# Variance products of two norms as four 64x64 tiles, with one logarithm and one exponential for both, and a new order of work

## The reference

```python
x1 = x + layernorm(attention(x)) * n1g + n1b
y  = x1 + layernorm(fc2(gelu(fc1(x1)))) * n2g + n2b
# layernorm(v) = (v - mean(v)) / sqrt(var(v) + 1e-5), over the 64 channels
```

## Time and profile before

| | |
|---|---|
| median of 3 runs | 8857.75 us (8851.5 to 8859.13) |
| profiled execution: time | 8850.95 us |
| profiled execution: span | 8849.2 us |
| mean granted TensorE clock | 0.967 |
| TensorE matmul busy | 8401.3 us, 95% |
| ScalarE busy | 6230.1 us, 70% |
| VectorE busy | 5742.6 us, 65% |
| GpSimd busy | 5155.6 us, 58% |

### The profile page before, as it was taken

How to read it: one execution, slowest core, us unless ns; L and a number is a source line. 1 busy time by engine, 2 the same in 40 slices (tenths; PEclk the granted TensorE clock), 3 DMA queues, 4 the chain that set the end, 5 groups by cost and what they waited for, 6 DMA issues and landing times.

```text
span 8849.2 us, 652880 instructions
## 1 busy us (share of the span) xinstructions
PE 8401.3 (95%) x291636; PEld 5471.0 (62%) x291636; DVE 5742.6 (65%) x8029; ACT 6230.1 (70%) x8530; POOL 5155.6 (58%) x5127
## 2 busy tenths in 40 slices
PE   8799999999999999999999999999999999878686
PEld 5556666666666666666666666666666666557565
DVE  1457777777777777777777777777777777222121
ACT  1468888888888888888888888888888888322121
POOL 0357777777777777777777777777777777100000
PEclk9789999999999999999999999999999999889888
DMA  3111111111111111111111111111111111699999
GB/s 99 39 32 38 37 38 38 38 38 37 38 38 38 38 38 37 38 37 35 36 38 37 38 38 38 38 37 38 38 38 38 37 37 36 202 324 319 337 317 332
DMA packets 1105192, 700.01 MB, mean 79 GB/s; under 512 B 616850, under 2 KB 1026834, under 8 KB 1100948
## 3 DMA queue, kind: packets, MB, share of 16 engines
q1 hardware_dynamic: 1100484, 564.33, 23.9%
q10 hardware_dynamic: 4608, 134.22, 3.5%
HBM read 412.97 MB, written 285.21 MB: 79 GB/s over the span
## 4 chain that ended last, share of the span: by engine, by line
PE 93%; DMA 4%; issue 1%; SPq 0%; POOL 0%; DVE 0%; ACTq 0%; ACT 0%; POOLq 0%; DVEq 0%
PE ps L475 15%; PE ps L453 13%; PE ps L511 12%; PE ps L523 11%; PE ps L436 10%; PE ps L551 10%; PE ps L501 6%; PE ps L487 5%; PE ps L495 5%; PE ps L424 3%; DMA out<-arena 3%; PE ps L398 1%; PE ps L389 1%; PE ps L390 1%; SPq L262 0%
## 5 line engine op out<-in xcount | busy, mean ns | idle before, releaser
L475 PEld LDWEIGHTS ps<-arena 32*32 32x32 f32 x131072 | 1290.9, 104 | 541.8 <-issue 508.4
L475 PE MATMUL ps<-arena 32*32 32x16 f32 x131072 | 1425.4, 186 | 17.9 <-issue 12.6
L664 ACT ACTIVATE arena<-ps,arena 128x1024 f32<-128x1024 f32 x1024 | 1140.4, 1114 | 357.8 <-PE ps L523 205.9
L775 DVE TENSOR_TENSOR arena<-ps,arena 128x768 f32<-128x768 f32 x1024 | 962.1, 940 | 539.3 <-PE ps L436 539.3
L913 POOL TENSOR_TENSOR arena<-arena 128x512 f32<-128x512 f32 x512 | 536.9, 1049 | 1282.9 <-DVE arena L846 1009.9
L453 PEld LDWEIGHTS ps<-arena 32*32 32x32 f32 x131072 | 1167.1, 105 | 152.6 <-issue 152.6
L453 PE MATMUL ps<-arena 32*32 32x16 f32 x131072 | 1218.9, 180 | 34.3 <-issue 34.3
L960 POOL TENSOR_TENSOR arena<-arena 128x512 f32<-128x512 f32 x512 | 629.5, 1230 | 1037.6 <-DVE arena L827 1037.6
L551 PE MATMUL ps<-xch,amat 128*128 128x256 f32 x4096 | 924.6, 388 | 288.0 <-ACT arena L688 214.3
L511 PE MATMUL ps<-arena 64*128 64x512 f32 x4096 | 1178.9, 652 | 8.6 <-ACT arena L664 4.5
L922 POOL TENSOR_TENSOR arena<-arena 128x512 f32<-128x512 f32 x1024 | 1044.0, 1041 | 10.5 <-PE ps L475 10.4
(11 more groups left out here) (89 smaller groups left out, 14021.8 us busy)
## 6 DMA issues: line engine op xcount, KB each, us to landing
arena<-in_x SPq DMA_DIRECT2D x4096, 32.0 KB
y<-ystripe SPq DMA_DIRECT2D x256, 512.0 KB, 5.3
amat<-mix SPq DMA_DIRECT2D x512, 256.0 KB, 3.4
xch<-y SPq DMA_DIRECT2D x512, 256.0 KB, 4.0
out<-arena ACTq DMA_DIRECT2D x32, 4096.0 KB, 27.1
mix<-amat SPq DMA_DIRECT2D x64, 256.0 KB, 2.0
wri<-in_w_real SPq DMA_DIRECT2D x64, 64.0 KB, 1.8
wri<-in_w_imag SPq DMA_DIRECT2D x64, 64.0 KB, 1.9
```

What stands on the lines that cost most here:

```text
L475: ins = mm(PV[32 * h:32 * h + 32, b, c0:c0 + N], vexp[r, sl, h, :, :], pT[r, sl, h // 2, h % 2, :], start=True, stop=True, tile_position=( ...
L664: f(hT[kk], M, ACT.Gelu, bias=b1[:, kk:kk + 1]).then_inc(done, 1)
L775: tt(qkv[ring(g, 4)][:, :, 4 * pp:4 * pp + 4, :].rearrange("p w s n -> p s w n"), M.rearrange("p a (s n) -> p (a s) n", s=2)[:, :, 0:3 * C ...
```

## The change

- Both variances come in one piece, `variances(i4, i6)`: four 64x64 products on the four quarters of the array. For the first norm the halves of `sq1` are swapped before, by two DMAs of 128 KB that SP issues (`swap_halves`, four groups behind the load), so that its products use the off-diagonal quarters; the second norm's use the diagonal ones. The results go to banks 0 and 1.
- One logarithm and one exponential over 1024 columns (`logs`, `roots`) replace two of 512 each.
- PSUM is laid out anew: `MA` in banks 0 and 1 (turned input, variances, first half of the first layer), `MB` in 2 and 3 (qkv products, second half), `PV` in the lower halves of 4 and 5 with the scores in their upper halves, `D1` in 6 and `H2` in 7.
- The orders of TensorE, ScalarE, VectorE and GpSimd change. The two parts of `scores` now stand in different steps, the two of `first_layer` side by side; softmax and weighted sum come one step earlier. Waits follow the new layout.

```diff
+SWAP = 4
-        sq1, l1, r1, dn1, x1T = (carve(512) for _ in range(5))
-        sq2, l2, r2, dn2, yg = (carve(512) for _ in range(5))
+        sq1, sq1x, dn1, x1T = (carve(512) for _ in range(4))
+        ls, rts = carve(1024), carve(1024)
+        r1, r2 = rts[:, 0:512], rts[:, 512:1024]
+        sq2, dn2, yg = (carve(512) for _ in range(3))
...
-        M = ps[:, 0:2, :]
-        S = ps[:, 2, :]
-        PV = ps[:, 3:5, 0:256]
-        PA = ps[:, 3, :]
-        D1, H2, TR = ps[:, 5, :], ps[:, 6, :], ps[:, 7, :]
-        XT, V1, V2 = D1, TR, PA
+        MA, MB = ps[:, 0:2, :], ps[:, 2:4, :]
+        PV = ps[:, 4:6, 0:256]
+        D1, H2 = ps[:, 6, :], ps[:, 7, :]
+        VV = MA
+        V1, V2 = VV[:, 0, :], VV[:, 1, :]
+        XT = MA[:, 0, :]
+        def S(sl):
+            return ps[:, 4 + sl // 4, 256:512]
...
+            def swap_halves(g):
+                if there(g):
+                    need(sp, sq1_sb, g)
+                    for a in range(2):
+                        sp.dma_start(sq1x[a * C:a * C + C, :], sq1[(1 - a) * C:(2 - a) * C, :]).then_inc(sq1x_in, 16)
...
                     load_x(d * 2 + k // GPS, k % GPS, Group(d * 8, k))
+                    swap_halves(Group(d * 8, k - SWAP))
                     if k % GPS == 0:
                         store_y(d * 2 + (k // GPS - 3), Group(d * 8, k - 12 + GPS - 1))
...
-                        after(pe, (dn1_sb, i5), (xT_sb, before(g)))
+                        after(pe, (gelu0, i6), (logs_sb, i5, i7), (xT_sb, before(g)))
...
-                            need(pe, biased, before(g))
+                            after(pe, (oT_sb, i3), (biased, before(g)))
...
-                            after(pe, (l2_sb, i7), (oT_sb, before(g)))
+                            after(pe, (biased, i2), (oT_sb, before(g)))
...
-                        after(pe, (xT_sb, i0), (dn1_sb, before(g)))
+                        need(pe, dn1_sb, before(g))
...
-                def variance1(g):
-                    if there(g):
-                        need(pe, sq1_sb, g)
-                        need(pe, l1_sb, before(g))
-                        mm(V1, ones, sq1, start=True, stop=True).then_inc(var1_ps, 1)
...
+                def variances(g, h):
+                    if there(g) or there(h):
+                        need(pe, sq1x_in, g, 32)
+                        need(pe, sq2_sb, h)
+                        after(pe, (xT_sb, i0), (gelu0, i6), (logs_sb, before(g), before(h)))
+                        settled(pe)
+                        if there(g):
+                            for a in range(2):
+                                b = 1 - a
+                                ins = mm(V1[b * C:b * C + C, :], ones[a * C:a * C + C, a * C:a * C + C],
+                                         sq1x[a * C:a * C + C, :], start=True, stop=True, tile_position=(a * C, b * C))
+                        if there(h):
+                            for a in range(2):
+                                ins = mm(V2[a * C:a * C + C, :], ones[a * C:a * C + C, a * C:a * C + C],
+                                         sq2[a * C:a * C + C, :], start=True, stop=True, tile_position=(a * C, a * C))
+                        ins.then_inc(var_ps, 1)
...
-                            after(pe, (gelu1, i6), (qkvB_sb, i1), (qkvA_sb, i1), (gelu0, before(g)))
+                            after(pe, (logs_sb, i4, i6), (xT_sb, i0), (gelu0, before(g)))
...
                 turn_x(i0)
-                weighted(i4, 0, pvA_ps)
-                first_layer(i5, 0, fc1a_ps)
-                weighted(i4, 1, pvB_ps)
+                scores(i2, 1)
                 second_layer(i6, 0, fc2a_ps)
                 second_layer(i6, 1, fc2b_ps)
-                project(i4)
-                project_qkv(i0, 0, qkvA_ps)
-                variance2(i6)
-                variance1(i4)
-                project_qkv(i0, 1, qkvB_ps)
-                scores(i2, 0)
-                scores(i2, 1)
-                first_layer(i5, 1, fc1b_ps)
+                project_qkv(i0, 0, MB, qkvA_ps)
+                weighted(i3, 0, pvA_ps)
+                variances(i4, i6)
+                project_qkv(i0, 1, MB, qkvB_ps)
+                weighted(i3, 1, pvB_ps)
+                first_layer(i5, 0, MA, fc1a_ps)
+                first_layer(i5, 1, MB, fc1b_ps)
+                scores(i1, 0)
+                project(i3)
...
+                def logs(g, h):
+                    if there(g) or there(h):
+                        event(act, var_ps, g)
+                        lo, hi = 0 if there(g) else 512, 1024 if there(h) else 512
+                        f(ls[:, lo:hi], VV.rearrange("p a n -> p (a n)")[:, lo:hi], ACT.Ln, bias=eps).then_inc(logs_sb, 1)
+
+                def roots(g, h):
+                    if there(g) or there(h):
+                        event(act, logs_sb, g)
+                        need(act, dn1_sb, before(g))
+                        need(act, dn2_sb, before(h))
+                        lo, hi = 0 if there(g) else 512, 1024 if there(h) else 512
+                        f(rts[:, lo:hi], ls[:, lo:hi], ACT.Exp, scale=-0.5).then_inc(roots_sb, 1)
...
                 act.preload_act_table_set(EXP_SET)
-                exponent(i4)
-                log1(i5)
                 log_norm(i2)
-                root1(i5)
-                log2(i7)
                 root_norm(i2)
-                root2(i7)
+                square2(i7)
+                exponent(i3)
+                logs(i5, i7)
+                roots(i5, i7)
                 act.preload_act_table_set(GELU_SET)
-                gelu(i6, 1, fc1b_ps, fc2b_ps, gelu1)
+                keep_o(i4)
+                gelu(i6, 0, MA, fc1a_ps, fc2a_ps, gelu0)
+                square(i1)
+                square1(i4)
+                gelu(i6, 1, MB, fc1b_ps, fc2b_ps, gelu1)
                 keep_x(i0)
-                square(i1)
-                keep_o(i4)
-                gelu(i5, 0, fc1a_ps, fc2a_ps, gelu0)
-                square2(i6)
-                square1(i4)
...
-                turn_q(i2)
                 sum_squares(i1)
-                turn_k(i2)
                 clamp(i1)
-                qkv_out(i0, 0, qkvA_ps, qkvA_sb)
-                sum_prob(i3)
-                invert(i3)
-                qkv_out(i0, 1, qkvB_ps, qkvB_sb)
+                bias(i2)
+                maximum(i2)
+                qkv_out(i0, 0, MB, qkvA_ps, qkvA_sb)
+                sum_prob(i2)
+                turn_k(i1)
+                qkv_out(i0, 1, MB, qkvB_ps, qkvB_sb)
+                invert(i2)
+                turn_q(i1)
                 normed1(i4)
-                turn_prob(i3)
+                turn_prob(i2)
                 normed2(i6)
                 add1(i4)
-                bias(i2)
-                maximum(i2)
                 gain2(i6)
...
                 add_o2(i5)
-                expand_v(i3)
-                divide(i3)
+                shift(i2)
+                scale_norm(i1)
                 norm_k(i1)
+                norm_q(i1)
+                divide(i2)
+                expand_v(i2)
                 add_o1(i0)
-                scale_norm(i1)
-                norm_q(i1)
                 add2(i6)
-                shift(i2)
```

More of the change, by code:

```diff
@@ L219, in need, with event, need2 @@
                 eng.wait_ge(s, g.base * per + (g.off + 1) * per)
+        def event(eng, s, g):
+            eng.wait_ge(s, g.base + (g.off + 1))
+        def need2(eng, s, h):
+            if there(h):
+                event(eng, s, before(h, -2))
         def after(eng, *users):
-            for s, g in users:
-                if there(g):
-                    need(eng, s, g)
+            for s, g, *h in users:
+                if there(g) or h and there(h[0]):
+                    event(eng, s, g)
                     return
@@ L329, in _ @@
                 load_x(i // GPS, i % GPS, Group(i, 0))
+                swap_halves(Group(i, -SWAP))
                 if i % GPS == 0 and i >= 12:
@@ L334, in _ @@
                     load_x(d * 2 + k // GPS, k % GPS, Group(d * 8, k))
+                    swap_halves(Group(d * 8, k - SWAP))
                     if k % GPS == 0:
                         store_y(d * 2 + (k // GPS - 3), Group(d * 8, k - 12 + GPS - 1))
-            for i in range(G, G + 9, GPS):
-                store_y((i - 12) // GPS, Group(i - 12, GPS - 1))
+            for i in range(G, G + 9):
+                swap_halves(Group(i, -SWAP))
+                if i % GPS == 0:
+                    store_y((i - 12) // GPS, Group(i - 12, GPS - 1))
             for i in range(2):
@@ L430, in project_qkv @@
                             need(pe, xT_sb, g)
-                            after(pe, (gelu0, i5), (gelu1, i6), (qkvB_sb, i1), (qkvA_sb, before(g)))
+                            after(pe, (gelu1, i6), (qkvB_sb, i1), (qkvA_sb, before(g)))
                         else:
-                            after(pe, (qkvA_sb, i0), (gelu0, i5), (gelu1, i6), (qkvB_sb, before(g)))
```

(23 more changed lines are left out.)

42 lines of the change are left out of this document (16 added, 26 removed).

## The result

The changed kernel takes 8755.27 us (median of 4 runs, 8750.57 to 8764.51) against 8854.62 before; the ratio is 0.9891 with a 95% interval of 0.9879 to 0.9903. It is faster, as forecast, but by 99 us where 287 were forecast, and 8755 lies above the range (8450 to 8730).

What follows compares the result with a forecast made beforehand. TensorE's matmul order was taken as the main loop's clock: 14.01 us a group becomes 13.34 of work plus a 0.11 wait, 13.45. Saving 0.56 x 512 = 287 us from 8857.75 gave 8571 us, range 8450 to 8730.

Steps and rivals of the forecast that it cites:

- Step 1: TensorE's variances: four quarter products run together, 1.06 us in place of 1.91, a gain of 0.85 a group.
- two rounds: Rival at the variances: the four products run in two turns, 0.86 us more a group, 9011 us; chance 0.10.
- Steps 2: TensorE's scores split in two places: 1.22 us each, 2.45 in all, 0.19 more a group.
- 3: TensorE's neighbours: first layers together gain 0.19 us; project, no longer behind the second layer, loses 0.19.
- Step 4: ScalarE behind the variances: scores wait for keep_o, 4.26 us against 4.15 of TensorE work, so 0.11 a group.
- Step 5: ScalarE otherwise: merging saves 0.27 us on logarithms and 0.19 on exponentials; all other work hidden by 0.9 or more.
- Step 6: Swap of halves in SP's queue: price 0, with 1.5 us cover for the swap and 1.5 to 2 for load_x.
- Step 7: VectorE and GpSimd: the same work in another order, in time for TensorE; price 0.
- Outside the loop: Filling and emptying the pipeline: would change by a few us at most.
- another wait or dearer halves: Rival in the main loop: dearer scores halves, slower handover, or late swap or turn_q; 13.81 us a group, 8755 us; chance 0.21.

Runs made afterwards that it cites:

- experiments 3: The changed kernel with two full 128x128 products for the variances and no swap, all else kept: 9135.79 us, ratio 1.032.
- 7: The changed kernel with keep_o ahead of the table load, stores ahead of the swap, two full 128x128 variance products and no swap: 8888.35 us, ratio 1.0035.
- Experiment 10: The changed kernel with one more counting step of TensorE's sequencer between the wait for keep_o and the first scores: 8774.98 us, ratio 0.9907.
- keep_o_first: The changed kernel with keep_o ahead of the table load instead of behind it: 8581.32 us, ratio 0.9693.
- Experiment 5: The changed kernel with SP's order load_x, store_y, swap in place of load_x, swap, store_y: 8689.78 us, ratio 0.9805.
- both_orders_full: Same run as 7: the changed kernel with keep_o and the stores moved ahead, two full variance products and no swap: 8888.35 us.
- experiment 11: The kernel before with the input loaded for the first group alone, so its values are wrong: 8708.26 us, ratio 0.9831.
- 8: The kernel before with eight more DMAs of 64 bytes a group, issued by SP ahead of load_x: 8762.98 us, ratio 0.9891.
- 9: The changed kernel with keep_o ahead of the table load, stores ahead of the swap, and four loads issued in pairs after the weighted parts: 8441.24 us, ratio 0.953.

## Why the prediction was wrong

The mechanism of the forecast is right: the products run together, and the scores wait for `keep_o`. Its sizes failed, in steps 1, 4 and 6. By its own steps, against the chain of the changed kernel:

- *The price of the kernel before.* The sum took 14.01 us a group from rows 2; the period is 13.99 (rows 3 had it). So 0.02 of the 0.56, 10 us, was no gain at all.
- *Step 1, variances.* The mechanism is right: 1.12 us, no two rounds, and experiments 3 and 7 price the second stream at 0.85, as forecast. The term was 0.06 small, and the counting step ahead of the products adds a gap of 0.07 that I had not charged: 0.13 together. By the rule that I gave from the Trainium skill (TensorE: Matmul & The Clock Gate, Part 3) the piece would have been 1.92; the trace does not agree with that use of it, since two pairs of these tiles share their rows.
- *Steps 2 and 3, scores and neighbours.* Right within 0.04 each.
- *Step 4, the wait for keep_o.* The mechanism is right, and so is ScalarE's part (4.16 us for 4.14). The handover is mis-sized: 0.12 us charged, 0.22 at the upper bound, 0.25 measured. I took it from a product of wide tiles that carries its wait itself; here two semaphore steps of the sequencer, the wait and behind it the counting step, stand between `keep_o` and the first product. Experiment 10 shows one more such step at 0.15 us at this place.
- *Step 5.* Right: in keep_o_first and after it, nothing else of ScalarE stands in the chain.
- *Step 6, SP's queue.* Failed. I gave load_x a cover of 1.5 to 2 us at a price of 0; every fourth group it comes late, because eight issues behind two stores take 8.1 us and not 5.4 (and 5.7 alone: they start 0.72 us apart, and I had divided the row of four by four). The step with the stores costs more all over. Experiment 5 puts it at 0.13 us a group, 0.05 of it the wait of `turn_x` and the rest in small products. The swap itself is hidden, as said.
- *Step 7.* Right, no wait for VectorE or GpSimd is in the chain.
- *Outside the loop.* A gain of 44 us in the first and last steps, forecast at nothing.

The sum: 13.45 forecast. Counting gap 0.07, variance piece 0.06, handover 0.13, ScalarE 0.03, other pieces together -0.02: 13.72, the 13.73 of the group shown. Stores 0.13: 13.85, against 13.88 measured. So the 0.56 of gain a group became 0.11 (0.02 for the price before, 0.43 for the new kernel), 287 us became 56, and the ends gave 44 back. The period of 13.88 is outside the 13.2 to 13.7 that the prediction gave as its bounds.

The rival "another wait or dearer halves" gave 8755 us, the measured number, and that is luck. Its handover 0.1 slower did come (0.13), but the halves were not dearer and the swap was not late, and of its 102 us the loop saved 56; the ends made up the rest. The point it had right is that small terms at the handovers add up on a cycle.

## What to carry to other kernels

When a wait is made part of the cycle that sets the period, the semaphore steps behind it are on the cycle too; price the handover from a row of the same kind of instruction, or move the producer so that the wait has slack. What such a step costs in the period must be measured: 0.15 us more at the handover was 0.04 in the period here. Here moving one ScalarE instruction ahead of a table load was worth 174 us and reordering SP's queue a further 114, both more than the change itself. Where a queue issues everything, follow the issue that comes last in the worst step, not in the mean one.

## What the runs showed of the hardware

- Four 64x64 tiles, each sharing its rows of the array with one other and its columns with another, all with moving data of their own, ran together: 1.12 us for 512 columns in two passes, against 1.10 for one full product at the same place (both_orders_full).
- DMAs of 32 KB and more slow TensorE's streams of small products though they share no data: 1.25 and 1.38 us on average for 64 products with the loads, 1.19 without (experiment 11), in single breaks of about 0.13 us, 0.7 to 1.0 us behind an issue. Stores and swaps make them too. Wide products show none of it: each qkv piece takes 0.850 to 0.851 us in all 286 groups. Eight 64-byte DMAs made no break, and delaying the loads by 2.4 us took 99 us off the kernel before. What in a DMA makes the break stays open: it is not any issue as such (8), and keeping half of the issues out of those pieces did not cure it (9).
- The same eight issues of SP took 5.7 us alone and 8.1 behind two 512 KB stores.
- In the first steps, which are unrolled code that runs once, a step is longer than in the loop, and it got shorter by more than the loop did. The table loads of the first 600 us, before and after:

```profile
L674 ACT ACT_TABLE_LOAD  x19: 1283/1283/1283, 263.6 to 597.4; - x19
```

```profile
L698 ACT ACT_TABLE_LOAD  x21: 1283/1283/1283, 263.0 to 591.6; - x21
```

333.8 / 18 = 18.5 us a step and 328.6 / 20 = 16.4. TensorE's clock differs there too (columns as in rows 3, before and after):

```profile
500.00:600.00 100.00, 88.99 (x2841) 50.46 (x2832) 52.55 (x76) 58.16 (x80) 49.96 (x51) 0.75 0.12 27
```

```profile
500.00:600.00 100.00, 92.35 (x3533) 56.82 (x3532) 68.35 (x92) 71.36 (x90) 60.96 (x62) 0.91 0.21 48
```

From 260 to 600 us the granted clock is 0.72 on average before and 0.81 after: it goes up and down between its two levels, 2.4 and 1.2 GHz, and is at the lower one for 191 us of the 340 before and 126 after. A first layer takes 2.01 us at the lower level and 1.06 at the higher (chain of the kernel before, at 398.98 and 441.45 us). If TensorE sets the pace there, half of the difference, 32 us, is an estimate of what the clock gave back, about the 33 us by which the first 20 steps became shorter. Whether the clock is the cause of the shorter steps or their consequence was not tried.
